# Rows of the second FFN's first groups prepared within attention, on GpSimd and ScalarE

## The reference

```python
x = x + _L1_xattn_ref(_layernorm(x, axis=-1), ctx_1024, ctx_1024, mask, Wq, bq, Wk, bk, Wv, bv, Wo, bo)
x = x + _L1_ffn_ref(_layernorm(x, axis=-1), gate_w, up_w, down_w, s_in, s_in_down)
# within the FFN, for x, for the weights and for the hidden rows, in blocks of 16 features:
sc8 = clip(max|x_block| / 6 * scale, 0, 448) rounded to eight bits
q   = x_block / (sc8 / scale) clipped to 6 and rounded to four bits
out = q * (sc8 / scale)
hidden = silu(gate_out) * up_out
```

## Time and profile before

| | |
|---|---|
| time, median of 3 runs | 706.92 us (706.83 to 707.96) |
| profiled execution | 708.72 us |
| its span, first to last instruction | 706.6 us |
| PE, VectorE, ScalarE, GpSimd busy | 81%, 72%, 53%, 30% |
| mean granted TensorE clock | 0.918 |

### The profile page before, as it was taken

The page is one execution under the profiler, slowest core; times in us unless marked ns, Lnnn a source line. Parts: engine busy times, 40 slices in busy tenths (PEclk is TensorE's granted clock), DMA queues, the critical chain, the costliest instruction groups (busy, mean ns, idle before and its releaser), DMA issues.

```text
span 706.6 us, 14547 instructions
## 1 busy us (share of the span) xinstructions
PE 569.6 (81%) x4543; PEld 417.5 (59%) x4552; DVE 505.7 (72%) x1418; ACT 377.0 (53%) x717; POOL 213.2 (30%) x243
## 2 busy tenths in 40 slices
PE   5399999609999999976799999997535876687677
PEld 3188888509998898864466666664212453355345
DVE  6358887695655556573456666666769999999987
ACT  1324443113343333323666777778765878785674
POOL 5725774524665455552121443310000000000000
PEclk9789999959999999996899999999757999999999
DMA  8884443269466655607000000000000000000001
GB/s 317 271 221 132 129 150 119 71 217 387 148 220 200 204 180 179 207 28 241 1 2 0 0 0 0 0 1 2 4 1 0 31 15 16 31 30 16 16 30 60
DMA packets 35540, 68.49 MB, mean 97 GB/s; under 512 B 5581, under 2 KB 24542, under 8 KB 34464
## 3 DMA queue, kind: packets, MB, share of 16 engines
q1 hardware_dynamic: 28816, 52.37, 22.8%
q0 software_dynamic: 5520, 13.61, 5.6%
q10 hardware_dynamic: 1152, 1.88, 0.9%
HBM read 53.78 MB, written 15.80 MB: 98 GB/s over the span
## 4 chain that ended last, share of the span: by engine, by line
PE 42%; DVE 23%; ACT 13%; issue 8%; DMA 8%; SPq 4%; POOL 2%; DVEq 0%; POOLq 0%; ACTq 0%
PE quad L1128 10%; DVE hh L2234 5%; ACT nPT L874 4%; PE quad L1193 3%; PE bank L1264 3%; PE quad L1476 3%; DMA early<-in_W 3%; DMA x_after_ffn<-row,niU 2%; PE bank L1202 2%; ACT hqT L1022 2%; PE quad L1306 2%; PE quad L1283 2%; DVE nM L2081 2%; PE quad L1467 2%; DMA X<-x_after_ffn 2%
## 5 line engine op out<-in xcount | busy, mean ns | idle before, releaser
L777 ACT ACTIVATE hid<-quad,early 128x128 f32<-128x128 f32 x156 | 44.5, 368 | 83.8 <-PE quad L1193 83.8
L1193 PE MATMUL quad<-xts,early 128*128 128x128 f32 x624 | 74.9, 279 | 4.3 <-DMA early<-in_W 4.0
L1193 PEld LDWEIGHTS quad<-xts,early 128*128 128x128 f32 x624 | 73.2, 195 | 6.6 <-issue 5.0
L1202 PE MATMUL bank<-W2s,hid 128*128 x312 | 70.5, 379 | 0.0
L1202 PEld LDWEIGHTS bank<-W2s,hid 128*128 128x128 f32 x312 | 57.8, 190 | 7.1
L598 POOL DMA_INDIRECT x_after_ffn<-row,niU x39 | 38.9, 999 | 58.0 <-DVE row L1861 41.5
L1476 PE MATMUL quad<-uT,xqT 128*128 128x512 bf16 x128 | 40.1, 417 | 19.8 <-DVE hh L2234 18.9
L1856 DVE SCALAR_TENSOR_TENSOR row<-bank,sco,row 128x256 f32<-128x256 f32 x39 | 18.6, 476 | 46.1 <-PE bank L1202 45.7
L998 ACT ACTIVATE sil<-quad,gmx 128x512 f32<-128x512 f32 x64 | 41.0, 686 | 18.8 <-PE quad L1467 18.2
L2081 DVE TENSOR_REDUCE nM<-quad 128x32 f32<-128x2048 f32 x16 | 36.7, 2292 | 18.5 <-PE quad L1283 18.5
L564 POOL DMA_INDIRECT rows_by_expert<-row,pi x38 | 37.8, 996 | 33.8 <-DVE pi L1698 23.1
(11 more groups left out here) (365 smaller groups left out, 1325.0 us busy)
## 6 DMA issues: line engine op xcount, KB each, us to landing
early<-in_W SPq DMA_DIRECT2D x37, 514.0 KB, 5.5
row<-rows_by_expert SPq DMA_DIRECT2D x38, 134.0 KB, 2.2
early<-in_ctxO SPq DMA_DIRECT2D x4, 1024.0 KB, 8.0
ctxs<-in_ctxT SPq DMA_DIRECT2D x4, 1024.0 KB, 13.7
W2s<-in_W SPq DMA_DIRECT2D x8, 512.0 KB, 3.6
X<-x_after_ffn SPq DMA_DIRECT2D x7, 516.0 KB, 7.3
out<-yo SPq DMA_DIRECT2D x14, 256.0 KB, 2.1
early<-in_W ACTq DMA_DIRECT2D x2, 514.0 KB, 8.9
```

The source lines that it names most:

```text
L777: ins = act.activation(hid[:, u, c * P:(c + 1) * P], bank[2 + u][:, c * P:(c + 1) * P], ACT.Gelu, bias=W1r[:, k, DC * H2 + c:DC * H2 + c + 1])
L1193: ins = pe.matmul(bank[2 + u][:, n * P:(n + 1) * P], W1r[:, m % RING, c * H2 + n * P:c * H2 + (n + 1) * P], xt[:, u, c, :], start=c == 0, ...
L1202: ins = pe.matmul(bank[6 + u % 2][:, 0:D], hid[:, u, c * P:(c + 1) * P], W2s[:, bass.ds(ex, 1), c, :].rearrange("p o s -> p (o s)"), start ...
```

## The change

Normalising the rows of groups 0 to 3 moves to GpSimd, in its batches 6, 7, 12 and 13. The last multiplication of the eight weight parts moves from VectorE to GpSimd. ScalarE makes absolute values and copies of groups 0 to 2 within batches 7 to 13, and those of group 3 in the first FFN group. VectorE sizes and quantises groups 0 and 1 and sizes group 2 within batches 8 to 14. Groups 2 and 3 are quantised ahead of `group(0)`, which then prepares no rows; `group(g)` for g from 1 to 4 prepares rows of group g+3. The statistics are closed in four parts instead of three, there are four quantised row buffers instead of two, and the loops over weight batches on ScalarE, GpSimd and VectorE are written out.

```diff
-        done_parts = [slice(1, 9), slice(9, NTILE - 3), slice(NTILE - 3, NTILE + 1)]
+        done_parts = [slice(1, 9), slice(9, 17), slice(17, NTILE - 3), slice(NTILE - 3, NTILE + 1)]
 # GpSimd
+            def rows_normed(g):
+                pool.wait_ge(s_nm2, 4 + g // 2)
+                if g > 1:
+                    pool.wait_ge(s_ax, g + 1)
+                pool.sem_inc(s_idle, 1)
+                for u in range(4):
+                    t = g * 4 + (u + 1)
+                    ins = pool.tensor_scalar(x4s[g % 2][:, u * D:(u + 1) * D], X2[:, t, 0:D], rs2[:, t:t + 1], nm2[:, t:t + 1],
+                                             ALU.mult, ALU.add)
+                ins.then_inc(s_x4, 1)
+            def weight_quantised(k):
+                pool.wait_ge(s_wrd, k + 1)
+                pool.sem_inc(s_idle, 1)
+                for to, src, m in zip(weight_slot(k, wq), weight_part(wb1), weight_blocks(k, wblkb)):
+                    ins = pool.tensor_tensor(to, src, m, ALU.mult)
+                ins.then_inc(s_wq, 1)
-                def batch(b, h, p, k=None):
+                def batch(b, h, p, k=None, q=None):
                     keys_in(p, b + 2, h)
+                    if q is not None:
+                        weight_quantised(q)
                     biased(b + 2)
+                for b in range(6, NB - 2):
+                    batch(b, b % 2, b // 2 + 1, k=b - 4 if b - 4 < SLOTS else None, q=b - 6 if b - 6 < SLOTS else None)
+                    if b in (6, 7, 12, 13):
+                        rows_normed((6, 7, 12, 13).index(b))
 # ScalarE, attention
+                    if b in (5, 9):
+                        done_roots(b // 9)
+                    if b in (7, 8, 13):
+                        rows_size({7: 0, 8: 1, 13: 2}[b])
                     inverse_sums(b)
+                    if b in (9, 10, 13):
+                        rows_half({9: 0, 10: 1, 13: 2}[b])
                     if stage == 2:
-                        rows_halved(0, 0)
-                        rows_normed(1, 1)
                         weights_out(4)
-                done_roots(1)
+                weights_out(5)
                 done_roots(2)
                 act.activation(tscr[:], tscr[:], ACT.Silu)
-                weights_out(5)
 # ScalarE, FFN
             x_out(0)
-            rows_halved(1, 1)
             for u in range(4):
                 silu(u, u, first=u < 2)
                 if u:
                     hidden_half(u - 1, u - 1)
+                if u == 1:
+                    rows_size(3)
+                    rows_half(3)
             hidden_half(3, 3)
-            act.wait_ge(s_nm2, 5)
-            tile_norm(2, 2)
-            act.wait_ge(s_xq, 2)
-            tile_norm(3, 3)
+            act.wait_ge(s_nm2, 6)
                 if i + 4 < NGR:
-                    tile_norm(i + 4, i + 4)
+                    tile_norm(i + 4)
 # VectorE, attention
-                for to, src, m in zip(weight_slot(k, wq), weight_part(wb1), weight_blocks(k, wblkb)):
-                    ins = tt(to, src, m, ALU.mult)
-                ins.then_inc(s_wq, 1)
+                def rows_between(b):
+                    if b == 6:
+                        done_scales(done_parts[0], 1, stn)
+                    if b == 8:
+                        rows_sizes(0, stn)
+                    if b == 9:
+                        done_stats(1)
+                        rows_sizes(1, stn, two_c[1])
+                    if b == 10:
+                        block_scales(both_c, stn)
+                    if b == 11:
+                        rows_quantised(0, stn)
+                    if b == 12:
+                        done_scales(done_parts[1], 2, stn)
+                        rows_scaled(1, stn, two_c[1])
+                        clamped(xf, stn)
+                    if b == 13:
+                        rows_rounded(1, stn, two_c[1])
+                    if b == 14:
+                        rows_sizes(2, stn)
 # VectorE, FFN
+            sized = [1, 2, 5, 7] + [2 * g + 1 for g in range(4, NTILE // 4)]
+            def rows_sizes(g, steps, c=rows_c):
+                v.wait_ge(s_ax, sized[g])
+                halves(absx[g % 2], halfx, 16, NBX // 16, big[:, c], steps)
                 if rows:
-                    rows_sizes(g + 2, g + 2, st)
+                    rows_sizes(g + 3, st)
                 hidden_sizes(g, st)
                 block_scales(slice(0 if rows else NBX, NBX + NBH), st)
                 if rows:
-                    rows_scaled(g + 2, st)
-                    rows_quantised(g + 2, st)
+                    rows_quantised(g + 3, st)
-            rows_sizes(1, 1, st)
-            product(0, 0)
-            product(1, 1)
-            block_scales(rows_c, st)
-            rows_scaled(1, st)
-            rows_quantised(1, st)
-            product(2, 2)
-            product(3, 3)
+            for u in range(4):
+                product(u, u)
+                if u == 1:
+                    rows_sizes(3, st, two_c[1])
+                    block_scales(both_c, st)
+            for g in (2, 3):
+                rows_quantised(g, st, two_c[g - 2])
             for g in range(NTILE // 4 - 1):
-                group(g, g + 2 < NTILE // 4)
+                group(g, 1 <= g and g + 3 < NTILE // 4)
```

More of the change, by code:

```diff
@@ L316, in two_layers_kernel @@
         nMT = sb("nMT", [P, S], BF16, en)
+        xqs = [sb(f"xq{k}", [P, 4, D], BF16, en) for k in range(1, 4)]
         en.close()
@@ L683, in _ @@
                     weight_scaled(k)
+                    weight_quantised(k - 1)
+                weight_quantised(SLOTS - 1)
+                for g in range(4):
+                    rows_normed(g)
         @block.scalar
@@ L818, in weights_out, with rows_size, rows_half @@
                 act.copy(to, bank[6][:].bitcast(BF16).rearrange("p (c o) -> p c o", c=DC if t < 4 else FT)).then_inc(s_wTe, 1)
[L820 to L827, removed]
-                act.wait_ge(s_x4, g + 1)
[L829 to L834, removed]
+            def rows_size(g):
+                act.wait_ge(s_x4, g + 1)
+                act.activation(absx[g % 2], top(x4s[g % 2]), ACT.Abs).then_inc(s_ax, 1)
+            def rows_half(g):
+                act.copy(xb[g % 2], top(x4s[g % 2])).then_inc(s_ax, 1)
             def done_roots(part):
-                act.wait_ge(s_dst, part + 1)
-                r = done_parts[part]
+                act.wait_ge(s_dst, part + 1 if part < 2 else 4)
+                r = done_parts[part] if part < 2 else slice(17, NTILE + 1)
                 act.activation(sd2[:, r], mv2[:, r, 1], ACT.Ln, bias=epsc[:, 0:1]).then_inc(s_dsd, 1)
@@ L941, in _ @@
                 batch(6, 0, p=3, k=1)
[L942 to L945, removed]
+                for b in range(7, NB - 2):
+                    batch(b, b % 2, p=(b + 1) // 2, k=b - 5 if b - 5 < SLOTS else None)
                 batch(NB - 2, 0, p=NB // 2 - 1, stage=1)
                 batch(NB - 1, 1, stage=2)
-                done_roots(1)
+                weights_out(5)
                 done_roots(2)
                 act.activation(tscr[:], tscr[:], ACT.Silu)
-                weights_out(5)
             with act.Else():
@@ L976, in _ @@
                     weights_out(t)
[L977 to L982, removed]
+                for part in range(3):
+                    done_roots(part)
+                for g in range(2):
+                    rows_size(g)
+                for g in range(2):
+                    rows_half(g)
+                act.wait_ge(s_xq, 1)
+                rows_size(2)
+                rows_half(2)
                 act.activation(tscr[:], tscr[:], ACT.Silu)
@@ L1013, in _, with tile_norm @@
                     hidden_half(u - 1, u - 1)
+                if u == 1:
+                    rows_size(3)
+                    rows_half(3)
             hidden_half(3, 3)
-            act.wait_ge(s_nm2, 5)
-            tile_norm(2, 2)
-            act.wait_ge(s_xq, 2)
-            tile_norm(3, 3)
+            act.wait_ge(s_nm2, 6)
+            def tile_norm(g):
+                act.wait_ge(s_xq, g - 1)
+                for u in range(4):
+                    t = g * 4 + (u + 1)
+                    ins = act.activation(x4s[g % 2][:, u * D:(u + 1) * D], X2[:, t, 0:D], ACT.Identity,
+                                         bias=nm2[:, t:t + 1], scale=rs2[:, t:t + 1])
+                ins.then_inc(s_x4, 1)
+                rows_size(g)
+                rows_half(g)
             def hidden_out(g, u, banks=(6, 0, 6, 6)):
@@ L1963, in each_block @@
                 return ap.unsqueeze(2).broadcast_to([P, t, BLOCK, ap.shape[2]])
[L1965 to L1967 removed]
+            two_c = [rows_c, slice(NBX, 2 * NBX)]
+            both_c = slice(0, 2 * NBX)
+            sized = [1, 2, 5, 7] + [2 * g + 1 for g in range(4, NTILE // 4)]
+            def rows_sizes(g, steps, c=rows_c):
+                v.wait_ge(s_ax, sized[g])
+                halves(absx[g % 2], halfx, 16, NBX // 16, big[:, c], steps)
             def hidden_sizes(g, steps):
```

(8 more changed lines are left out.)

97 lines of the change are left out of this document (46 added, 51 removed).

## The result

The changed kernel took 730.37 us, median of 4 runs (727.88 to 731.06), against 707.44 (706.83 to 708.74) of the kernel before: a ratio of 1.0315 with a 95% interval of 1.0285 to 1.0345. The forecast was 729.5, range 721 to 740, slower.

The account below looks back on a forecast made before the run. No single engine bounds the whole; VectorE sets the FFN groups' time, a ring across engines attention's. Terms 3.9 - 3.0 - 0.2 - 4.0 + 28.0 - 2.1 = +22.6 on 706.92 gave 729.5 us, range 721 to 740.

Parts of the forecast that it names:

- The stall: FFN groups 1 to 4: VectorE waits 7.0 us a group for ScalarE's absolute values; +28.0 us, bounds 25.2 and 28.
- The rival in which ScalarE is ahead in time: FFN groups: ScalarE has rows g+3 ready when VectorE asks, so groups cost nothing; 701.5 us, chance 0.10.
- Attention: Attention batches: ScalarE's row steps 2.3 plus GpSimd's normalising 1.6; +3.9 us, bounds 0 and 7.1.
- the copy: Attention batches 9, 10: ScalarE's rows_half delays the maxima copy 0.5 us each; with rows_size in 13 about 1.1.
- the absolute values alone in 7 and 8: Attention batches 7 and 8: ScalarE's rows_size ahead of the inverse sums makes the maxima copy late, 0.1 us each.
- GpSimd's normalising: Attention batches 6, 7, 12, 13: one meeting a batch with VectorE's maxima steps, 0.4 each; 1.6 us, bounds 0 and 4.8.
- VectorE's new inserts: Attention: row sizes, scales, quantising and statistics scaling, at most about 2.5 us a batch, covered by idle time; costed at nothing.
- The seam: End of attention to first gates: ScalarE no longer normalises and halves rows 0 and 1; -3.0 us, bound 0.
- Gates to last product: First gates to last product before group 0: quantising leaves, sizing of rows 3 comes; -0.2 us, bounds -0.5 and +1.
- To group 0: Last product before group 0 to its first: idle 5.1 and sizing 1.3 go, quantising 2.3 comes; -4.0 us.
- group 5: FFN group 5 loses its row work and takes 21.6 instead of 23.7 us; -2.1 us.
- Group 6: FFN group 6: predicted change 0.

Follow-up runs that it names:

- Experiment 1: Changed kernel with VectorE's FFN groups preparing rows g+2 again instead of g+3, all else as changed; 701.74 us, ratio 0.9902 to the kernel before.
- experiment 2: Changed kernel, still rows g+3, with ScalarE normalising at its group's head and making absolute values before the last hidden half; 701.73 us, ratio 0.9908 to the kernel before.
- experiment 3: Changed kernel with ScalarE's tile_norm directly behind the last hidden_half, ahead of x_out and two hidden_out; 716.58 us, ratio 1.0118 to the kernel before.
- experiment 5: Experiment 1 with ScalarE's row copies moved to waits in batches 13 to 15, VectorE's and GpSimd's row work correspondingly later; 699.65 us, ratio 0.9886 to the kernel before.
- experiment 4: Changed kernel with only the weights' last multiplication moved back from GpSimd to VectorE; 728.81 us, ratio 1.0285 to the kernel before.
- Experiment 6: Experiment 1 with the PE's transposes of the first rows issued last inside attention's branch instead of behind it; 700.83 us, ratio 0.9888 to the kernel before.

## Why the prediction was right

**The stall (+28.0; measured +28.82).** Right in mechanism, place, number and size: four waits of 6.90 to 7.08, where 7.0 was worked out from ScalarE's list in the trace of before. Experiment 1 takes the wait away by asking later, experiment 2 by preparing earlier, and experiment 3 shortens it by what it shortens the list. Of the rest, 28.82 - 27.8 = 1.0, VectorE's own work makes 0.4 (busy 92.4 us in the four groups, 92.0 before), and other idle time of VectorE the other 0.6; the granted clock of group 1, a mean between the levels of 1.2 and 2.4 GHz, is 0.83 against 0.93 before, but that this is its cause was not tried. The rival in which ScalarE is ahead in time falls; at its 701.5 us the kernel arrives, at 701.74 and 701.73, once its condition is made true.

**Attention (+3.9; measured +2.1).** The term was mis-sized in both halves. ScalarE: the copy was to cost 0.5 in batches 9 and 10, and cost 0.29 and 0.33; with the absolute values 0.96 instead of 1.1 in batch 13; the absolute values alone in 7 and 8 nothing measurable (-0.05, +0.02) instead of 0.1 each. ScalarE in batch 9 of after, the row copy ahead of the copy of the maxima:

```profile
430.92 1.03 ACT L863 COPY ctxs<-x 128x1024 bf16<-128x1024 bf16 x1
431.85 0.36 ACT L899 COPY nMT<-bank 128x256 bf16<-128x256 bf16 x1
```

and the PE in batches 9 and 13:

```profile
431.02 1.08 PE L1301 MATMUL bank<-xt,WqS 128*128 128x256 f32 x4
432.27 0.29 PE L1341 MATMUL quad<-nMT,jslot 32*128 32x256 bf16 x4 [0.17 <-ACT nMT L899]
...
471.73 0.29 PE L1341 MATMUL quad<-nMT,jslot 32*128 32x256 bf16 x4 [0.79 <-ACT nMT L899]
```

The PE stands in its projections until 432.10, so of the late copy only 0.17 us shows as a wait; in batch 13 it waits 0.79. The sum took the start of the turned scores as the time when the copy was wanted, and the projections ahead of them were not looked at.

GpSimd's normalising was to meet VectorE's maxima steps at 0.4 a batch. VectorE's steps in batch 7:

```profile
410.28 0.47 DVE L2122 CAST nMb<-nM 128x32 bf16<-128x32 f32 x1
410.79 0.21 DVE L2123 TENSOR_TENSOR nMr<-nM,nMb 128x32 f32<-128x32 f32 x1
411.03 0.27 DVE L2124 CAST nMb<-nMr 128x32 bf16<-128x32 f32 x1
411.33 0.21 DVE L2125 TENSOR_TENSOR nMb<-nMr,nMb 128x32 bf16<-128x32 f32 x1
```

GpSimd beside them:

```profile
408.97 1.74 POOL L631 TENSOR_TENSOR ctxs<-wraw,ctxs 128x512 f32<-128x512 f32 x2 [0.17 <-ACT ctxs L851]
410.70 2.19 POOL L642 TENSOR_SCALAR ctxs<-X,rs,nm 128x256 f32<-128x256 f32 x4
```

Only the first step is held up, until the float multiplication ends at 410.71, and such a meeting was there before. The prediction misread this: it took the 0.19 us step at 432.92 for one of a batch without a meeting, but the step just ahead of it had met the same multiplication (which ends at 432.85):

```profile
432.25 0.64 DVE L2088 CAST nMb<-nM 128x32 bf16<-128x32 f32 x1
```

Beside the normalising the three other steps of batch 7 take 0.69 us together, and 0.56 in batches without it: 0.13 instead of the 0.4 forecast, and batch 6, with the same 0.13, grows by 0.14. Batch 7 doesn't grow (-0.05), since the multiplication there ends 6.23 us after the exponentials, 0.18 sooner than in before. A meeting can cost more: in batch 13 of after one step takes 0.48, but there ScalarE's copy is later still; in experiment 5 a step that takes 0.50 is on the path.

Batch 12 grows by 0.35, and this is the term that was costed at nothing: VectorE's new inserts. The maxima reduction there starts 3.94 us after the exponentials instead of 3.47, without the 0.67 us of idle time that it had before:

```profile
456.97 2.28 DVE L2115 TENSOR_REDUCE nM<-quad 128x32 f32<-128x2048 f32 x1
```

VectorE works through statistics and scaling of rows until 456.17, and the addition, which comes next, ends at 457.05. Two of the statistics' steps are slowed beside GpSimd's multiplication (last section): with that on VectorE (experiment 4) the batch takes 0.22 less, and in experiment 5 it is at 9.37 again.

Batch 5 grows by 0.22, which no term held. The first root steps of the statistics, 0.5 us, moved into it behind the exponentials; ScalarE's halving of the weights starts 0.44 later after the exponentials, GpSimd's float multiplication behind it ends 0.44 later (6.66 instead of 6.22 us), and the maxima step that it holds up ends at 6.71 instead of 6.26. Batch 11 is 0.16 shorter, and there the multiplication ends 0.16 sooner. Both are read from the traces; no experiment moved the roots.

**The seam (-3.0; measured -2.4).** The gain is there, and what was left out is the PE: its transposes start 2.90 us after its last work within the branch, and reach ScalarE 0.94 late. The trace of before couldn't show this: the same transposes stood 3.52 us behind the PE's last work there, but waited for VectorE's rows. Experiment 6 gives the forecast's length. **Gates to last product (-0.2; +0.39)**: the same code took 13.44 in experiment 1, so one execution doesn't settle a term of this size. **To group 0 (-4.0; -4.52) and group 5 (-2.1; -2.55)** held, 0.5 more each.

**Group 6 (0; +0.89).** Unedited. It has a clock of 0.85 and the PE is busy 18.50 us for the work that took 17.26 at 0.92. The same stretch in experiment 1:

```profile
656.74:679.17 22.43, 18.37 (x111) 11.18 (x112) 19.42 (x28) 14.74 (x19) 0.00 (x0) 0.85 0.07 25
```

and in experiment 2:

```profile
654.43:675.41 20.98, 16.93 (x111) 10.22 (x112) 19.42 (x29) 14.75 (x19) 0.00 (x0) 0.92 0.07 27
```

In the nine profiled executions it takes 22.4 to 22.6 us at 0.85 (five of them) and 21.0 to 21.6 at 0.92 (four), in kernels with and without the stall. So the length goes with the clock; why the clock falls there in some executions and not in others stays open.

That the total came out within 1 us is luck in the smaller terms: the stall alone was sized to 3%, and the overpriced attention (1.8) made up for what stall, seam and group 6 took beyond their forecast (0.8 + 0.6 + 0.9), with the rest adding to -0.4.

## What to carry to other kernels

When work is asked for one turn earlier, move its producer's place in its own list too, or show that the list gets there in time: read the time from the head of that list, and what releases the head. If the head waits for the very engine that now asks, the wait is the whole list from there, paid in every turn. And price a delayed link by when its reader is free, not by when it was last seen to start.

## What the runs showed of the hardware

**Behind a branch.** The PE's first instruction behind attention's branch starts 2.90 us after its last work inside it in after, and 3.46 in experiment 1 (2.8 to 3.5 in after and experiments 1 to 5), with no engine to wait for. Work placed as the last thing in the branch instead starts at once (experiment 6). Whether the first piece behind the branch is then as late, the runs don't show, since the gates wait for ScalarE's copy; nor do they say what the 3 us are.

**VectorE beside GpSimd.** Tiny VectorE steps took three to six times as long beside GpSimd's instructions with two tensor inputs. VectorE in batch 12:

```profile
453.13 0.68 DVE L1970 TENSOR_SCALAR rs<-rs,gmx 128x8 f32<-128x8 f32 x1
453.85 0.97 DVE L1971 SCALAR_TENSOR_TENSOR nm<-mv,rs 128x8 f32<-128x8 f32 x1
```

GpSimd there:

```profile
453.17 0.61 POOL L675 TENSOR_TENSOR nKB<-Kall,own 128x256 f32<-128x256 f32 x1 [3.39 <-PE quad L1343]
453.74 2.15 POOL L663 TENSOR_TENSOR wq<-ctxs 128x512 bf16<-128x512 f16 x2
```

With the multiplication on VectorE (experiment 4) these two steps take 0.23 and 0.17. Both sides lose: GpSimd's pair takes 2.15 here and 1.62 to 1.67 in six of the eight. The Trainium skill (SBUF — State Buffer, section "Who interferes with whom") has one of the two block until the other's instruction is through; here the first step ends at 453.81, 0.03 after GpSimd's expansion of keys at 453.78, and the second at 454.82, 0.03 after the first of the pair (1.05 us, to 454.79), which agrees; by the profile, though, the first step began 0.04 before the keys. Beside the normalising the trace agrees in part: the three steps of batch 7 don't show such a hold, but a step in batch 13 (0.48 us from 468.76) ends 0.04 after the normalising there, at 469.20, and the one in experiment 5 ends 0.03 after it. What decides between the two, the runs don't say.
